# Attention outputs by way of memory, value matmuls at a lag of two blocks, and row transfers with more outer entries

## The reference

```
x = x + layernorm(attn(layernorm(x)))            # 16 heads of 8, bias by relative position
x = x + layernorm(ffn(layernorm(x)))

attn: logits[b,h,l,m] = q.k * scale + bias[h, l-m];  out = softmax(logits) @ v
ffn:  y = x + softmax(q.k * scale) @ v @ w_proj      # the same shape of attention, no bias
      y = y + expert(argmax gate) of gelu MLP, 8 experts
```

## Time and profile before

| | |
|---|---|
| device time, median of 3 runs | 1099.91 us (1099.27 to 1103.8) |
| profiled execution: device time | 1094.4 us |
| its span, first to last instruction | 1092.3 us |
| stage 0, from its first unit to its last | about 87 to 558 us |
| stage 1 | about 621 to 968 us |
| PE busy / DVE / ACT / POOL | 80% / 71% / 59% / 13% of the span |
| mean granted PE clock, whole span | 0.906 of full speed |
| DMA share over stage 0 / over stage 1 | 0.26 / 0.18 |

### The profile page before, as it was taken

How to read it: one execution, slowest core, us unless ns; L and a number is a source line. 1 busy time by engine, 2 the same in 40 slices (tenths; PEclk the granted TensorE clock), 3 DMA queues, 4 the chain that set the end, 5 groups by cost and what they waited for, 6 DMA issues and landing times.

```text
span 1092.3 us, 25373 instructions
## 1 busy us (share of the span) xinstructions
PE 870.8 (80%) x9075; PEld 327.7 (30%) x9075; DVE 771.5 (71%) x1388; ACT 641.3 (59%) x1208; POOL 138.9 (13%) x376
## 2 busy tenths in 40 slices
PE   3328979998998999989946387999979999984871
PEld 2102323333332333323313011222322222243861
DVE  7356757776775777767358676899969999746544
ACT  6204646665665666656646066889869889941222
POOL 8100000000000000000010000000100100001772
PEclk9757989999998999999978588999989999996996
DMA  2722223233223223320002323321111110001123
GB/s 56 215 75 74 75 73 86 83 86 87 67 71 80 86 84 84 84 78 24 3 1 62 122 57 89 110 82 48 54 37 48 58 44 30 3 1 48 43 48 89
DMA packets 41965, 72.18 MB, mean 66 GB/s; under 512 B 9177, under 2 KB 28825, under 8 KB 41849
## 3 DMA queue, kind: packets, MB, share of 16 engines
q1 hardware_dynamic: 40018, 65.81, 21.3%
q0 software_dynamic: 1472, 3.02, 1.1%
q10 hardware_dynamic: 358, 1.76, 0.5%
HBM read 59.95 MB, written 10.62 MB: 65 GB/s over the span
## 4 chain that ended last, share of the span: by engine, by line
PE 49%; DMA 20%; DVE 9%; ACT 8%; issue 6%; SPq 4%; POOL 3%; DVEq 0%; ACTq 0%; POOLq 0%
PE bank L1118 16%; DMA maxima_rows<-max_rows 13%; PE bank L1166 13%; PE bank L1173 9%; ACT prob_mem L693 7%; PE bank L1110 6%; DVE unit_max L834 2%; DMA k_parts<-prob_mem 2%; POOL moe_out L616 2%; DMA q_rows<-maxima_rows 2%; DVE stats L750 2%; POOL prob_mem L605 1%; DVE norm L764 1%; SPq L392 1%; SPq L373 1%
## 5 line engine op out<-in xcount | busy, mean ns | idle before, releaser
L693 ACT ACTIVATE prob_mem<-bank 128x512 f32<-128x512 f32 x1024 | 555.3, 597 | 317.7 <-PE bank L1173 232.4
L831 DVE CUSTOM_DVE_ANT_0 y_res<-bank,tables 128x1024 bf16<-128x1024 f32 x256 | 312.3, 1224 | 158.6 <-PE bank L1110 149.5
L834 DVE TENSOR_REDUCE unit_max<-bank 128x1 f32<-128x1024 f32 x256 | 294.7, 1214 | 40.1 <-PE bank L1110 39.9
L1118 PE MATMUL bank<-prob_mem,v_ring 128*32 128x256 f32 x4096 | 315.2, 394 | 2.3 <-issue 1.7
L1110 PE MATMUL bank<-k_rows,q_rows 56*128 56x512 bf16 x512 | 164.0, 425 | 57.9 <-DMA k_rows<-k_parts 43.6
L1166 PE MATMUL bank<-q_rows,k_rows 59*128 59x512 bf16 x512 | 170.3, 401 | 44.8 <-DMA q_rows<-maxima_rows 26.2
L1166 PE MATMUL bank<-more_rows 59*128 59x512 bf16 x512 | 162.3, 389 | 28.2 <-DMA more_rows<-maxima_rows 15.1
L1173 PE MATMUL bank<-feat,flip 96*32 96x512 bf16 x2048 | 163.9, 395 | 0.0
L1110 PE MATMUL bank<-more_rows 56*128 56x512 bf16 x512 | 162.7, 392 | 0.0
L1118 PEld LDWEIGHTS bank<-prob_mem,v_ring 128*32 128x32 f32 x4096 | 107.1, 111 | 150.1 <-ACT prob_mem L693 58.7
L561 POOL CAST max_parts<-unit_max 128x8 bf16<-128x8 f32 x64 | 12.2, 191 | 809.6 <-DVE unit_max L831 463.5
(11 more groups left out here) (159 smaller groups left out, 565.4 us busy)
## 6 DMA issues: line engine op xcount, KB each, us to landing
tables<-bias_rows SPq DMA_DIRECT2D x30, 480.0 KB, 8.5
more_rows<-q_parts SPq DMA_DIRECT2D x32, 192.0 KB
more_rows<-k_parts SPq DMA_DIRECT2D x32, 192.0 KB
q_rows<-q_parts SPq DMA_DIRECT2D x28, 192.0 KB
k_rows<-k_parts SPq DMA_DIRECT2D x28, 192.0 KB
feat<-bias_parts SPq DMA_DIRECT2D x14, 378.0 KB
w_moe<-in_L_ffn_w_dram SPq DMA_DIRECT2D x16, 256.0 KB, 3.8
q_parts<-prob_mem SPq DMA_DIRECT2D x8, 384.0 KB, 3.2
```

The lines of the kernel that those rows point to most:

```text
L693: nc.scalar.activation(prob[:, ul % 2, kb, half * N:(half + 1) * N], b_bank(entry(ul, kb, half)), ACT.Exp).then_inc(exp_done[a], 1)
L831: nc.vector.tensor_tensor_reduce(out=no_use[qb % 2], in0=scores, in1=bias, scale=1.0, scalar=LEAST, op0=ALU.add, op1=ALU.max, accum_out=un ...
L834: nc.vector.tensor_reduce(unit_max[:, slot, qb:qb + 1], scores, AX.X, ALU.max).then_inc(max_done[1], 1)
L1118: ins = nc.tensor.matmul(AV[VM * c:VM * (c + 1), :], v_ring[:, head_slot, b * QB + kb, :], prob[:, ul % 2, kb, c * W:(c + 1) * W], start=( ...
```

## The change

- **Rows.** The 48-row q transfer becomes two of 24 rows with outermost size 24 (so `QK_DMAS` goes from 8 to 10 for each head). The skewed table is read with its outer two sizes exchanged, 32 first, and the 0/1 matrix `flip` is permuted to match.
- **Outputs.** `o_ring` (128 KB a unit) is stored to memory by SP (`store_sums`, ahead of `maxima_of` in the list). In the last body and after it SP loads the sums back as feature-major `o_all` and the denominators as `den_all` (`load_sums`). At a stage's end PE transposes them by groups of four tiles (`to_natural`), and DVE forms one reciprocal and one product per group (`natural`). The transposes and the scaling within units are gone, and the room for them is the freed half of `prob`.
- **Maxima.** ACT instead of DVE copies the transposed maxima to `max_rows`, after the exponentials of block 2. `maxima_t` moves behind the value matmuls of its block.
- **Values.** `weigh_v` stands once in every block, at a lag of two; block 2 no longer lacks it and block 3 no longer has two.

```diff
-        prob = prob_mem[:, :].rearrange("p (s k q) -> p s k q", s=2, k=QB)
+        prob = prob_mem[:, 0:QB * L].rearrange("p (k q) -> p k q", k=QB)
+        o_all = prob_mem[:, QB * L:QB * L + T]
+        den_all = prob_mem[0:H, QB * L + T:QB * L + 2 * T]
...
-            src = bass.AP(row.tensor, row.offset, [[2 * L, 3], [1, 32], [1, SKW]])
+            src = bass.AP(row.tensor, row.offset, [[1, 32], [2 * L, 3], [1, SKW]])
...
-                        sp.dma_start(ring[f * HP:f * HP + 6 * DH, lo:hi],
-                                     bass.AP(one.tensor, one.offset, pairs + [[1, hi - lo]])).then_inc(loaded, 16)
+                        if s == 0:
+                            for r in range(2):
+                                sp.dma_start(ring[f * HP + 3 * DH * r:f * HP + 3 * DH * (r + 1), lo:hi],
+                                             bass.AP(one.tensor, one.offset, [[T, 3 * DH], [1, hi - lo]])).then_inc(loaded, 16)
+                        else:
+                            sp.dma_start(ring[f * HP:f * HP + 6 * DH, lo:hi],
+                                         bass.AP(one.tensor, one.offset, [[T, 2 * DH], [0, 3], [1, hi - lo]])).then_inc(loaded, 16)
...
+            def store_sums(a, u, slot):
+                sp.wait_ge(o_ready[a], u + 1)
+                sp.dma_start(o_dram[bass.ds(u, 1)].rearrange("o p w -> (o p) w"), o_ring[:, slot, :]).then_inc(o_stored[a][slot], 16)
+
+            def load_sums(a, b, first, heads):
+                sp.wait_ge(o_stored[a][b], 16 * (first + heads + (heads > 1)))
...
+                if heads == 1:
+                    sp.dma_start(o_all[first * DH:(first + 1) * DH, b * L:(b + 1) * L],
+                                 bass.AP(unit.tensor, unit.offset, [[W, DH], [VM * W, 4], [1, W]])).then_inc(o_loaded[a][b], 16)
...
+                        if not (first and ul == 0):
+                            store_sums(a, u - 1, (ul - 1) % B)
                         if not (last and ul == UB - 1):
                             maxima_of(a, u + 1, ul + 1)
+                        if last and ul in (2, 3):
+                            load_sums(a, ul - 2, 0, H - UB // B)
+                        if last and ul >= 2:
+                            load_sums(a, ul % B, (u - 2) // B, 1)
...
+                load_sums(a, 0, H - 1, 1)
+                store_sums(a, U - 1, 1)
+                load_sums(a, 1, H - 1, 1)
...
+            def maxima_out(a, u, slot, src, stored):       # on ACT
+                act.wait_ge(max_t_mm[a], u + 1)
+                if stored:
+                    act.wait_ge(mrow_stored[a], 16 * (u - 1))
+                nc.scalar.copy(max_rows[:, slot, :], src).then_inc(max_copied[a], 1)
...
-                        if not (first and ul < 2):
-                            act.wait_ge(av_done[a], u - 1)
...
+            def natural(a, g):                              # on DVE
+                ts = slice(g * TG, (g + 1) * TG)
+                dve.wait_ge(natural_mm[a], g + 1)
+                nc.vector.reciprocal(recip[:, g % 2], bank[:, 4 + g % 2, 0:TG * H].rearrange("p (t h) -> p t h", t=TG)
+                                     ).then_inc(natural_recip[a], 1)
...
-                                    to_natural(a, u - 2, ul % 2, out_of(out_entry(ul)))
...
-                            elif kb > 2:
-                                if kb == 3:
+                            else:
+                                if kb == 2:
                                     before_av(a, UB // 4 * i, ul, not (first and ul == 0))
                                 pe.wait_ge(exp_done[a], 2 * (QB * u + kb - 2) + 2)
-                                for late in range(0 if kb == 3 else kb - 2, kb - 1):
-                                    weigh_v(a, ul, late, False)
+                                weigh_v(a, ul, kb - 2, False)
+                            if kb == MAX_AT and not no_max:
+                                b_bank_free(a, i, out_entry(ul), first, last)
+                                maxima_t(a, u + 1, (ul + 1) % 2, max_t(out_entry(ul)))
...
             pe.wait_ge(exp_done[0], 2 * QB * U)
+            for g in range(G // 2):
+                to_natural(0, g)
             for kb in (6, 7):
                 weigh_v(0, 3, kb, kb == 7)
-            to_natural(0, U - 1, 1, LAST_OUT)
-            pe.wait_ge(unit_scaled[0], U)
+            for g in range(G // 2, G):
+                to_natural(0, g)
+            pe.wait_ge(natural_done[0], G)
...
-            pe.wait_ge(unit_scaled[1], U - 1)
-            output_transposes(range(G // 2))
             pe.wait_ge(exp_done[1], 2 * QB * U)
+            for g in range(G // 2):
+                to_natural(1, g)
             for kb in (6, 7):
                 weigh_v(1, 3, kb, kb == 7)
+            pe.wait_ge(natural_done[1], G // 2)
+            output_transposes(range(G // 2))
             output_projection(range(G // 2))
```

More of the change, by code:

```diff
@@ L43, in sandwich_kernel @@
     KR = 7 * DH
-    QK_DMAS = 8
+    QK_DMAS = 10
+    SUM_LOADS = 5 + 2 * 4
     HP = P // 2
@@ L685, in body @@
                         u = UB * i + ul
[L686 to L687 removed]
                         for kb in range(QB):
                             if kb == 2 and not (first and ul < 1):
[L690 removed]
+                                evacuate(a, u - 1, (ul - 1) % 2, None if first and ul < 3 else 16 * (4 * i + (ul - 1) // 2))
                             for half in range(2):
                                 act.wait_ge(sb_done[a], 2 * (QB * u + kb) + half + 1)
[L693 removed]
+                                nc.scalar.activation(prob[:, kb, half * N:(half + 1) * N],
                                                      b_bank(entry(ul, kb, half)),
                                                      ACT.Exp).then_inc(exp_done[a], 1)
+                            if kb == MAX_AT and not (last and ul == UB - 1):
+                                maxima_out(a, u + 1, (ul + 1) % 2, max_t(out_entry(ul)), not (first and ul == 0))
                 body(0, first=True)
@@ L905, in add_projection @@
                 if g == G // 2:
-                    scale_unit(1, U - 1, H - 1, 1, 1, LAST_OUT)
+                    for late in range(G // 2, G):
+                        natural(1, late)
                     feature_major(2, None, range(G // 2, G), 2)
@@ L1098, in _, with to_natural @@
             projections(0, w_in_t[:, 2, :], w_in_t[:, 0, :], w_in_t[:, 1, :])
-            def to_natural(a, u, slot, out):
-                pe.wait_ge(o_ready[a], u + 1)
-                for half in range(2):
-                    ins = nc.tensor.transpose(out[:, half * P:(half + 1) * P], o_ring[:, slot, half * P:(half + 1) * P], ident[:])
-                ins.then_inc(unit_t_mm[a], 1)
+            def to_natural(a, g):
+                pe.wait_ge(o_loaded[a][g // (G // B)], 16 * SUM_LOADS)
+                if g >= 2:
+                    pe.wait_ge(natural_done[a], g - 1)
+                for tt in range(TG):
+                    t = g * TG + tt
+                    nc.tensor.transpose(bank[:, 4 + g % 2, tt * H:(tt + 1) * H], den_all[:, t * P:(t + 1) * P], ident[0:H, 0:H])
+                for tt in range(TG):
+                    t = g * TG + tt
+                    ins = nc.tensor.transpose(bank[:, g % 2, tt * P:(tt + 1) * P], o_all[:, t * P:(t + 1) * P], ident[:])
+                ins.then_inc(natural_mm[a], 1)
             def scores_a(slot, head_slot, b, qb, f):
@@ L1156, in b_bank_free @@
                     pe.wait_ge(exp_done[a], 2 * QB * u + half + 1)
-                else:
-                    if not (last and ul == UB - 1):
-                        pe.wait_ge(max_copied[a], u + 2)
-                    if not (first and ul < 2):
-                        pe.wait_ge(unit_scaled[a], u - 1)
+                elif not (last and ul == UB - 1):
+                    pe.wait_ge(max_copied[a], u + 2)
             def scores_b(a, ul, kb, f):
@@ L1193, in body @@
                         done = last and lu >= UB
-                        no_max, no_out = last and ul == UB - 1, first and ul < 2
+                        no_max = last and ul == UB - 1
                         pe.wait_ge(mrow_loaded[a][ul % 2], 32 * (4 * i + ul // 2 + 1))
```

87 lines of the change are left out of this document (36 added, 51 removed).

## The result

The changed kernel takes 998.95 us in the median of 4 runs (998.22 to 1000.97), against 1099.59 us for the kernel before (4 runs): ratio 0.908, 95% interval 0.905 to 0.911. It is faster by 9.2%. The profiled execution went from 1094.4 to 999.43 us. Of all the runs told of here, one (of the kernel with the q rows alone spread) fell into a slower state, 1141 us at a granted clock of 0.72, and is left out of its figures.

A forecast was written before the change was run, and what follows sets the result against it. PE and the maxima's round trip, delayed by row transfers on few engines, were taken to bound the stages. Terms -36 - 7 - 6 - 27 - 12 + 8 + 4.5 = -75.5 took 1099.9 to 1024 us, range 1003 to 1052.

The forecast's parts named there:

- What bounds the kernel: In the stages, PE and the maxima's round trip through memory, with stores held behind row transfers; 39.2 us lost in stage 0.
- Blocks 2 and 3: Both stages: fewer transposes and moved value matmuls save 0.92 us a unit in stage 0 (-27), 0.43 in stage 1 (-12).
- Row transfers in stage 0: Stage 0: rows spread over 12 or more engines leave queues empty by the next maxima store; -36 us of 39.2 lost.
- Stage 1's first units: Stage 1 from 633.73 to 730.65: 9.7 us lost over nine periods, part staying for expert weights; -6 us.
- The start: Ahead of the first maxima store: two more issues for each first set of rows cost SP some 1.1 us.
- the first store of stage 0 is on the chain too: First maxima store of each stage: 5.95 us becomes 1.3, 4.6 back less some 1.1 for issues; -7 us for both.
- The ends: Ends of both stages: uncovered round trip, transposes and products add 8 us in stage 0 and 4.5 in stage 1.
- The stores of the sums at nothing: Each unit: 128 KB stored ahead of the maxima may delay them 0.5 to 1 us, within the cover; cost nothing.
- The rival that they make the kernel slower: Sums' stores slow every maxima store; at 8.7 us each, stage 1 loses some 130 us, about 1150 us; chance 0.03.
- The signs named: Signs in the profile: loads under 2.5 us after stores, PE's maxima wait under 8 us, no clock below 0.9 within stages.
- From the profile to the median: Whole kernel: the median shown is 5.5 us above the profiled execution; the same offset was assumed after the change.

The follow-up runs named there:

- the runs with only one of the two edits: Kernel before with both row changes and value matmuls at a lag of two: 1008.0 us, 0.923; changed kernel with value matmuls as before: 1019.6 us, 0.934.
- the first two groups of runs: Follow-up runs came in three groups of four kernels, the last on another chip; the kernel before took 1091.3, 1091.3 and 1097.8 us beside them.

## Where the prediction was right, and which steps failed

*What bounds the kernel: right.* Row transfers on two and three engines held up the maxima's store. Undoing that alone brings most of the gain, doing all the rest without it makes the kernel slower, and the engines' shares show it. The rule of the Trainium skill that was cited (DMA: Bandwidth & Descriptors, "Why a DMA increments its semaphore by 16 and not by 1") agrees with the traces at both ends, 0.13 before and a share of 1.00 after. The twelve engines that it gives the q rows alone are not separated by any run.

*Blocks 2 and 3: right to a hundredth in the unit's time.* 12.54 us a unit in stage 0 (forecast 12.54: 9.12 + 3.42) and 9.26 in stage 1 (forecast 9.26). But part of the reason for stage 1 was read too simply. I costed it as PE's stall; in truth PE and DVE stood at the same limit, as the runs with only one of the two edits show, and the units in the middle of the stage took 9.76, not the 9.69 that I took from the one in the earlier trace rows.

*Row transfers in stage 0: -36 forecast, -32 measured* (402.6 - 345.5 = 57.1 over the 27 periods, of which 27 x 0.92 = 24.8 is the shorter unit). I put the whole 39.2 us down to slow stores. Seven of them are no slow stores and stayed: 5.4 in the unit at the loop's jump back, which takes 17.96 us after the change too, and 0.8 in each first unit of the second and the last body (13.33, which no run explains).

*Stage 1's first units: -6 forecast, -18 measured.* This is the step with the plainest mistake, and one of the two that put the forecast outside its range. I wrote of "nine periods" between 633.73 and 730.65; there are eight, so the loss was 96.9 - 77.5 = 19.4 us and not 9.7. I also kept 3.7 for the expert weights' loads, though the loss that stayed is at most 1.2 us. After the change:

```profile
562.42 0.29 SPq L424 DMA_DIRECT2D maxima_rows<-max_rows  x1
...
637.72 0.32 SPq L424 DMA_DIRECT2D maxima_rows<-max_rows  x1
```

The same eight periods take 75.3 us (8 x 9.26 is 74.1): -21.6, of which 8 x 0.43 = 3.4 is the shorter unit.

*The start: +1 forecast ahead of the first maxima store, -11.3 measured.* This is the other one. The forecast step "the first store of stage 0 is on the chain too" priced only the wait behind that store and added two issues. It missed that SP waits once more before that, for the parts of q and k to be stored, and that these stores queue behind the first rows and the first two skewed tables. SP in the kernel before, and in the changed one:

```profile
49.03 2.03 SPq L373 DMA_DIRECT2D k_parts<-prob_mem  x3
66.92 0.70 SPq L392 DMA_DIRECT2D q_rows<-q_parts  x1
```

```profile
49.77 2.23 SPq L375 DMA_DIRECT2D k_parts<-prob_mem  x3
58.61 0.71 SPq L395 DMA_DIRECT2D q_rows<-q_parts  x2
```

15.9 us of standing became 6.6 (7.4 with the table alone spread, 7.8 with the q rows alone, 6.2 with both). The row was there to be read: the chain of waits showed 16.4 us for those stores, and I passed over it since nothing in the diff touches them. The first maxima stores themselves gave 1.9 and 2.2 us rather than the 4.6 reckoned for each. The two further issues cost nothing: the q and k rows of one head take 4.5 us to issue (58.61 to 63.13) where they took 4.8.

*The ends: +12.5 forecast, +16.4 measured.* End of stage 0 after the change:

```profile
481.98 1.08 ACT L737 ACTIVATE prob_mem<-bank 128x512 f32<-128x512 f32 x2 [0.82 <-PE bank L1207]
...
486.12 0.37 ACT L707 COPY o_ring<-bank 128x256 f32<-128x256 f32 x1 [3.06 <-PE bank L1155]
...
486.52 0.37 SPq L434 DMA_DIRECT2D unit_sums<-o_ring  x1
...
488.58 0.59 SPq L449 DMA_DIRECT2D prob_mem<-unit_sums  x1
490.67 0.50 PEld L1138 LDWEIGHTS bank<-ident,prob_mem 16*128 16x128 f32 x4 [5.10 <-DMA prob_mem<-unit_sums]
...
494.47 0.54 DVE L860 RECIPROCAL recip<-bank 128x64 f32<-128x64 f32 x1
...
496.56 1.15 DVE L799 BATCH_NORM_AGGREGATE meanvar<-stats 128x2 f32<-128x6 f32 x16
```

From 483.06 to 496.56 it is 13.5 us against 4.4: +9.1 (forecast +8). The round trip, 486.49 to 490.67, took 4.2 us (forecast 4.6). What was too small is the pair of reciprocal (128x64, 0.54) and product, 1.2 to 1.3 where 1.05 stood in my sum, and PE's transposes: 1.9 for the first two groups where I had 1.5, and 1.7 for the group after the wait where I had 0.7. The granted clock there, from 490 to 492 us, is 0.50. Stage 1:

```profile
857.49 4.12 ACT L737 ACTIVATE prob_mem<-bank 128x512 f32<-128x512 f32 x8 [0.23 <-PE bank L1200]
...
881.89 1.15 DVE L799 BATCH_NORM_AGGREGATE meanvar<-stats 128x2 f32<-128x6 f32 x16
```

861.61 to 881.89 is 20.3 us against 13.0: +7.3, forecast +4.5.

*The stores of the sums at nothing: right, as far as can be told.* The rival that they make the kernel slower needs a maxima store of about 6 us in every unit of stage 1; with four times the stores most took 1.4 and the slowest 3.2.

*The signs named.* PE's matmuls waited 41.3 us for the maxima rows before (the 26.2 of the earlier trace rows and 15.1 for the rows of the other buffers) and not at all after, its weight loads 0.4, where under 8 was asked. Loads did not follow their store within 2.5 us in every unit (up to 3.5), but PE did not wait for them. Clock below 0.9 within the stages is left at their starts and behind the loop's jump.

*From the profile to the median.* The profiled execution before lay 5.5 us under its median, and I took that along. After the change the profiled one lies at its median, so 5 of the 25 us are not in any step.

Where the profiles' 94.7 us lie, step by step (us):

| step | forecast | measured |
|---|---|---|
| start of stage 0, up to its second store | -3.5 | -13.2 |
| start of stage 1, from the last statistics to its second store | -3.5 | -5.0 |
| row transfers, 27 periods of stage 0 | -36 | -32.3 |
| row transfers, first units of stage 1 | -6 | -18.2 |
| blocks 2 and 3, and the rest of the units, stage 0 | -27 | -29.9 |
| the same, stage 1 | -12 | -16.9 |
| the two ends | +12.5 | +16.4 |
| expert layer (111.3 to 115.7) | 0 | +4.4 |
| sum | -75.5 | -94.7 |

The last row but one is not the change's doing. With the same expert layer it took 108.4 to 112.5 us in the profiles of the first two groups of runs and 115.8 to 117.8 in those on the other chip. Without it the steps would lie further still below the forecast. So the two large misses, 9.7 at the start and 12.2 in stage 1's first units, make up all of the 19.2 us and more, and the others nearly cancel. That they cancel is luck. The range was too narrow on the fast side: it came from bounds of the terms that I had, and the two largest misses were a count and a term that I did not have.

## What to carry to other kernels

Here a transfer's outermost size set how many engines carried it (2: a share of 0.13; 24 and 32: shares up to 1.00), and a 6 KB store issued behind it took 7 to 12 us instead of 1.3. Look for a DMA share that stays at one or two sixteenths, and then list every wait in the kernel that stands behind such a transfer, not only the one on the main path. Where two engines have nearly the same period (9.69 and 9.76 here), relieving one of them shows next to nothing: make both edits before you judge either. And an edit that shortens units turns hidden transfers into waits, so clear the queue first; with the queue left as it was, the same edits lost 2% here. When you forecast, list the waits ahead of the first unit too, and count the periods.

## What the runs showed of the hardware

A hardware loop's jump back cost one unit of each stage 4.3 to 6.1 us, with PE idle for 3.2 us for nothing that the profile shows and at a granted clock of 0.51 after it; written out, the kernel was 1% faster. Two sets of transfers on two and three engines held up the same small stores, and in stage 0 spreading either one did most of the work (-23 and -34 us alone, -32 together): the single effects on the kernel (-29 and -61 us) do not add up to the joint one (-66). Two engines moved 53 GB/s, 26 each, while sixteen at a share of 1.00 moved 186, 11.6 each. Four stores of 128 KB issued within 1.9 us put only 0.1 us on the 6 KB store behind them in stage 1.
